# First pair's scan in PSUM with its sums on TensorE, the last attention in tiles and banks of its own, and another order of clearing and loading at the start

## The reference

```
h = exp(dt * A) * h + dt * B * x ;  y = sum over states of h * C ;  y = (y + x * D) * silu(z)
```

## Time and profile before

| | us |
|---|---|
| median of 3 runs | 2176.59 (2176.43 to 2183.86) |
| the profiled execution | 2186.44 |
| its span | 2184.6 |

### The profile page before, as it was taken

The page is one execution under the profiler, slowest core; times in us unless marked ns, Lnnn a source line. Parts: engine busy times, 40 slices in busy tenths (PEclk is TensorE's granted clock), DMA queues, the critical chain, the costliest instruction groups (busy, mean ns, idle before and its releaser), DMA issues.

```text
span 2184.6 us, 17479 instructions
## 1 busy us (share of the span) xinstructions
PE 1713.5 (78%) x6245; PEld 983.5 (45%) x6245; DVE 1372.9 (63%) x1516; ACT 651.0 (30%) x983; POOL 1016.5 (47%) x708
## 2 busy tenths in 40 slices
PE   2024354347999987999999979999998899999885
PEld 1011121014564543665555635655465466664552
DVE  3497799954467996648899956568997300124224
ACT  1003133112424333333344333423532322222210
POOL 1788855877752347775643477863343000000000
PEclk7556565568999997899999979999999799999557
DMA  8453202023531132343311332432121012210000
GB/s 167 110 140 95 63 20 70 24 75 104 132 101 35 44 82 64 88 116 87 97 46 52 81 95 86 114 95 77 29 58 44 0 44 63 54 44 10 1 0 10
DMA packets 174926, 148.43 MB, mean 68 GB/s; under 512 B 137972, under 2 KB 138360, under 8 KB 174840
## 3 DMA queue, kind: packets, MB, share of 16 engines
q1 hardware_dynamic: 147192, 71.78, 13.7%
q0 software_dynamic: 27648, 75.53, 12.2%
HBM read 132.01 MB, written 15.24 MB: 67 GB/s over the span
## 4 chain that ended last, share of the span: by engine, by line
PE 54%; DVE 23%; issue 5%; ACT 4%; DMA 1%; POOL 0%; DVEq 0%; SPq 0%; ACTq 0%; POOLq 0%
PE ps L801 39%; PE ps L804 10%; DVE tiles L1387 4%; DVE tiles L1380 4%; DVE tiles L1395 3%; DVE slot L1334 2%; PE ps L1016 2%; DVE slot L1338 1%; PE ps L846 1%; DMA mring<-mixing 1%; ACT tiles L619 1%; DVE sampled L1345 1%; ACT tiles L716 1%; ACT tiles L621 1%; DVE normal L1278 1%
## 5 line engine op out<-in xcount | busy, mean ns | idle before, releaser
L565 POOL DMA_INDIRECT slot<-corners,index x576 | 723.1, 1255 | 271.3 <-issue 163.3
L801 PE MATMUL ps<-toep,tiles 128*128 128x512 f32 (+3 forms) x2048 | 589.6, 436 | 4.2 <-DMA mring<-mixing 1.9
L801 PEld LDWEIGHTS ps<-toep,tiles 128*128 128x128 f32 x2048 | 368.8, 191 | 232.1 <-issue 134.0
L581 POOL TENSOR_TENSOR tiles<-tiles 128x1024 f32<-128x1024 f32 x120 | 291.3, 2427 | 355.9 <-DVE tiles L1387 343.0
L1387 DVE TENSOR_TENSOR_SCAN tiles<-tiles 128x1024 f32<-128x1024 f32 x128 | 301.2, 2353 | 12.3
L700 ACT COPY tiles<-ps 128x512 f32<-128x512 f32 x256 | 149.6, 585 | 466.3 <-PE ps L801 466.0
L801 PE MATMUL ps<-tiles,sel 96*128 96x512 bf16 x512 | 162.7, 442 | 137.6 <-DVE tiles L1395 116.1
L804 PE MATMUL ps<-tiles,mring 128*128 128x128 f32 (+2 forms) x1024 | 243.8, 381 | 0.0
L801 PE MATMUL ps<-tiles 128*128 128x64 f32 (+5 forms) x770 | 197.1, 401 | 36.1 <-ACT tiles L716 17.6
L685 ACT ACTIVATE tiles<-tiles,negA 128x1024 f32<-128x1024 f32 x128 | 146.8, 1149 | 233.6 <-DVE tiles L1387 212.7
L804 PEld LDWEIGHTS ps<-tiles,mring 128*128 128x128 f32 x1024 | 167.2, 191 | 77.5 <-issue 66.0
(11 more groups left out here) (231 smaller groups left out, 1772.6 us busy)
## 6 DMA issues: line engine op xcount, KB each, us to landing
toep<-in_phi_pad_dram SPq DMA_DIRECT2D x64, 513.0 KB, 4.0
mring<-mixing SPq DMA_DIRECT2D x128, 128.0 KB, 4.4
slot<-corners,index POOLq DMA_INDIRECT x576
corners<-turned SPq DMA_DIRECT2D x128, 64.0 KB, 1.9
corners<-tiles SPq DMA_DIRECT2D x4, 648.0 KB, 4.9
residual<-in_x_dram SPq DMA_DIRECT2D x4, 512.0 KB, 3.9
mixing<-tiles SPq DMA_DIRECT2D x8, 256.0 KB, 4.5
out_dram<-residual SPq DMA_DIRECT2D x4, 512.0 KB, 2.7
```

Source lines behind the costliest of these rows:

```text
L565: g.indirect_dma_start(out=slots[number % 3][:, k, :, :].rearrange("p a c -> p (a c)"), out_offset=None, in_=tables[h], in_offset=bass.Ind ...
L581: g.tensor_tensor(f(Y[h]), f(Y[h]), f(HC[n % 2]), ALU.add).then_inc(*ysum.up())
L801: return t.matmul(o, w, r, start=start, stop=stop)
```

## The change

- **The beginning.** VectorE clears only the two tiles that serve as zeros for the tables, and the offset weights; POOL clears all other weight tiles before its first gather. SyncE loads x, constants, offset weights and bias, fills the tables with zeros, writes the tables of pair 0 as soon as x is turned, and only then loads mixing weights and all the rest. ScalarE loads its function table before the first wait. Folding the convolution taps into `win` is a unit of its own, one setup step earlier.
- **Scan of pair 0.** The input product is written over the B row in ps[2], and the scan reads it there. TensorE adds the products HC into ps[0] by multiplying with the identity, and finish_y reads ps[0]. The B row of the next state waits for the scan, not for the input product. VectorE's order is scan s, product s, input s+1. POOL does nothing for this scan. Pairs 1 to 3 are as before.
- **Heads.** Exp, Ln and step sizes are done by halves of 512 columns, and the x projection of a half waits only for its own half of the convolution.
- **Last attention.** D of pair 3 becomes stage E with buffers and semaphores of its own: ps[0] and ps[1], tiles 0 to 5, 10, 18 and 19. It waits for its own layer norm alone.
- **Order.** TURNS is written anew for all engines. On POOL pair 0 and pair 1 gather in one run (A288), then come the 32 sums of pair 1. On VectorE seven groups of pair 1 (two before) stand ahead of the last finish_y of pair 0. On TensorE, D of pair 2 goes on behind the spectral stage of pair 3, interleaved with E: at "variance 3" of pair 3, blocks 0 to 10 of pair 2's 16 row blocks have been begun and the rest follows (before, all of them and its experts up to the thirteenth were ahead). The units between the marks in the middle are the same, in another interleaving.

```diff
-        A122 B A3 B A3 B A4 B A4 B A4 B A4 B10 A4 B A3 B A B A B A B A B A B A B A B A B A B A B A B A2 B A122 B32 A123 B
+        A288 B32 A121 B A3 B A B A B A6 B A4 B A4 B A4 B25 A124 B A2 B4 A10 B A4 B A4 B25""",
...
             for s in range(N_STATE * h, N_STATE * h + N_STATE):
+                if j == 0:
+                    pe += [("b rows", j, s), ("c rows", j, s)] + ([("sum", j, s - 1)] if s % N_STATE else [])
+                    dve += [("scan", j, s), ("product", j, s)]
...
+        def in_place(j):
+            return j == 0
...
+        attentions = (Attention(0, 0, 6, 7, 8, (11, 12), 13, 15, 16, 17, 9, ps[2], ps[3]),
+                      Attention(1, PAIRS - 1, 0, 1, 2, (3, 4), 19, 10, 3, 18, 5, ps[0], ps[1]))
...
+            load(xs(0)[:], x_v[0], xin_in)
             load(cst[:], consts, early)
-            load(xs(0)[:], x_v[0], xin_in)
+            for h, r in enumerate(image):
+                load(F[r, 16, 0:TAPS * 18].rearrange("p (k o) -> p k o", o=18), w_off, early)
             load(boff[:], bcast_row(b_off), early)
             sp.wait_ge(*zeroed.at(0, 1))
...
             def load_rest():
+                sp.wait_ge(*weights_zeroed.at(0, 1))
+                for tile, m in ((0, M_plus), (4, M_minus)):
+                    load(...)
...
+            for tile in (wmain, win, wout, wqkv2, wqkv3, wrouter, wexp, bexp, mar, mring[0], mring[1]):
+                g.memset(tile[:], 0.0)
+            for n in range(2):
+                last = g.memset(normal[n][:, 0:2], 0.0)
+            last.then_inc(*weights_zeroed.up())
             pool.wait_ge(*ready.at(0, 1))
...
-                pe.wait_ge(*x1_ok.at(j, 2 * h + 2))
+                pe.wait_ge(*x1_ok.at(j, 2 * h + q + 1))
...
+                read = scan_ok if in_place(j) or s == 0 else bin_ok
+                if some(read.at(j, s)):
+                    pe.wait_ge(*read.at(j, s))
                 wide(ps[2], sel[:, n, :], bcs[h]).then_inc(*b_ps.up())
...
+            def sum_states(j, s):
+                h, n = s // N_STATE, s % N_STATE
+                pe.wait_ge(*hc_ok.at(j, s + 1))
+                if n == 0 and h == 1:
+                    pe.wait_ge(*y2_ok.at(j, 1))
+                for q in range(2):
+                    last = t.matmul(sums[:, HALF * q:HALF * q + HALF], ident, F[:, HC[n % 2], HALF * q:HALF * q + HALF],
+                                    start=n == 0, stop=n == N_STATE - 1, skip_group_check=True)
+                last.then_inc(*first_sum.up())
...
             def query_or_key(j, n):
                 if n == 0:
                     pe.wait_ge(*ld1.ok.at(j, 1))
                     if j + 1 < PAIRS:
                         pe.wait_ge(*y2_ok.at(j + 1, 2))
-                    else:
-                        pe.wait_ge(*out_ok.at(j - 1, 1))
...
-                v.tensor_tensor(f(DBX[s % 2]), f(DTX[s // N_STATE]), ps[2][:], ALU.mult).then_inc(*bin_ok.up())
+                to = ps[2][:] if in_place(j) else f(DBX[s % 2])
+                v.tensor_tensor(to, f(DTX[s // N_STATE]), ps[2][:], ALU.mult).then_inc(*bin_ok.up())
...
-                v.tensor_tensor_scan(f(HS), f(DA[s % 2]), f(DBX[s % 2]), 0.0, ALU.mult, ALU.add).then_inc(*scan_ok.up())
+                given = ps[2][:] if in_place(j) else f(DBX[s % 2])
+                v.tensor_tensor_scan(f(HS), f(DA[s % 2]), given, 0.0, ALU.mult, ALU.add).then_inc(*scan_ok.up())
```

More of the change, by code:

```diff
@@ L85, in at, with __init__, up @@
     def at(self, j, n):
-        return self.sem, j * self.per_pair + n
-STAGES = "AHBCD"
+        return self.sem, (j - self.first) * self.per_pair + n
+class Part:
+    def __init__(self, event, earlier):
+        self.event, self.earlier = event, earlier
+    def up(self):
+        return self.event.up()
+    def at(self, j, n):
+        return self.event.at(j, self.earlier + n)
+STAGES = "AHBCDE"
 BANK_UNITS = ("fold", "average", "turn x", "offsets", "turn offsets", "turn", "turn last", "conv samples", "x in", "z in", "rows", "step",
@@ L99, in one_of_each, with place_of @@
     return [(name, j, 0) for name in names]
+def place_of(j):
+    return 1 if j == PAIRS - 1 else 0
 class Plan:
@@ L113, in __init__ @@
             self.spectral(j, *(of[e]["C"] for e in ("PE", "DVE", "ACT", "SP")))
-            self.attention(j, *(of[e]["D"] for e in ("PE", "DVE", "ACT", "SP")))
+            self.attention(j, *(of[e]["DE"[place_of(j)]] for e in ("PE", "DVE", "ACT", "SP")))
         self.stages = of
@@ L142, in sampling @@
                 act += [("copy last", j, m // 2)]
+            if j == 0 and m == 4:
+                dve += [("fold taps", 0, 0)]
             if j == 0 and 1 <= m <= 6:
@@ L157, in heads @@
             pe += both("x in") + both("z in") + both("rows") + both("step")
-            act += both("silu x") + both("silu z") + both("copy rows") + both("soft") + [("exp ln", j, h)]
-            dve += both("split rows") + [("step sizes", j, h)]
+            act += both("silu x") + both("silu z") + both("copy rows")
+            for q in (2 * h, 2 * h + 1):
+                act += [("soft", j, q), ("exp ln", j, q)]
+            dve += both("split rows") + both("step sizes")
     def scan(self, j, pe, dve, act, pool):
@@ L1106, in work @@
                     c_rows(j, m)
+                if unit == "sum":
+                    sum_states(j, m)
                 if unit == "out":
@@ L1167, in _ @@
             boot = lambda ins: (ins.then_inc(*boot_v.up()), dve.wait_ge(*boot_v.at(0, boot_v.raised)))
-            for tile in (woff, wmain, win, wout, wqkv2, wqkv3, wrouter, wexp, bexp, mar, mring[0], mring[1]):
-                v.memset(tile[:], 0.0)
-            v.memset(F[:, 17:19, :], 0.0)
+            v.memset(F[:, 17:19, :], 0.0).then_inc(*zeroed.up())
+            v.memset(woff[:], 0.0).then_inc(*zeroed.up())
             v.memset(eps, 1.0e-5)
-            for n in range(2):
-                last = v.memset(normal[n][:, 0:2], 0.0)
-            last.then_inc(*zeroed.up())
+            dve.wait_ge(*zeroed.at(0, 2))
             dve.wait_ge(*early.at(0, early.raised))
@@ L1392, in product @@
                 dve.wait_ge(*c_ps.at(j, s + 1))
-                if some(ysum.at(j, s - 1)):
-                    dve.wait_ge(*ysum.at(j, s - 1))
-                v.tensor_tensor(f(Y[h]) if n == 0 else f(HC[n % 2]), f(HS), ps[3][:], ALU.mult).then_inc(*hc_ok.up())
+                if some(summed(j, s - 1)):
+                    dve.wait_ge(*summed(j, s - 1))
+                to = f(Y[h]) if n == 0 and not in_place(j) else f(HC[n % 2])
+                v.tensor_tensor(to, f(HS), ps[3][:], ALU.mult).then_inc(*hc_ok.up())
             def finish_y(j, h):
-                dve.wait_ge(*ysum.at(j, N_STATE * (h + 1)))
-                link(v.scalar_tensor_tensor(out=f(Y[h]), in0=f(XC[h]), scalar=dskip, in1=f(Y[h]), op0=ALU.mult, op1=ALU.add))
+                dve.wait_ge(*summed(j, N_STATE * (h + 1)))
+                link(v.scalar_tensor_tensor(out=f(Y[h]), in0=f(XC[h]), scalar=dskip, in1=sums[:] if in_place(j) else f(Y[h]),
+                                            op0=ALU.mult, op1=ALU.add))
                 v.tensor_tensor(f(Y[h]), f(Y[h]), f(SZ[h]), ALU.mult).then_inc(*y2_ok.up())
```

399 lines of the change are left out of this document (212 added, 187 removed).

## The result

The changed kernel takes 2108.52 us (median of 4 runs, 2099.8 to 2110.8) where the kernel before, run beside it, takes 2180.23 (2176.43 to 2183.99): a ratio of 0.9664, 95% interval 0.9628 to 0.97, or 71.7 us less. The forecast was 2080, 98 us less, with a range of 2040 to 2128; the narrower range that it gave its own mechanism, 2060 to 2100, was missed.

What follows compares the result with a forecast made beforehand. VectorE was taken to bound the first pair, TensorE the middle, a chain of dependent short steps the last attention. +3 - 36 + 0 - 41 - 24 = -98 us against the median 2176.59 gave 2079, rounded to 2080; range 2040 to 2128.

Steps and rivals of the forecast that it cites:

- -36: First spectral stage, between first and second output projection: becomes bound by TensorE, 349 against 384.7 us; bounds 0 and -50.
- -41: Pair 3's saturated spectral stage: shortens as 38 to 48 us of pair 2's attention work on TensorE moves behind it.
- 0 for the middle: Two middle periods, 837.4 to 1683.5 us: same units, only interleaving and halved heads change; bounds -20 and +15.
- the halved heads: Before the first scan: x projection needs half the convolutions, 2 us; halved softplus steps 1 us; first scan step near 194.5.
- the 13 us for late B rows: First pair's scan: B rows queue behind sums on TensorE, 0.4 us per state over 32 states; bounds 0 and 29.
- the guess from the product rows: First pair's scan: a PSUM operand costs nothing, as for the input product (1202 ns with, 1225 without).
- the step given: First spectral stage: pair 1's gathers start near 330, end near 550, its scan near 710, so TensorE bounds the stage.
- -24: Last normalisation to the end: two attention streams in separate banks and tiles take 152 us against 175.9; bounds 125 and 199.
- rival (a): The tail keeps 1.2 GHz and the two streams hinder each other in queues: 199 instead of 152, total 2127; chance 0.13.

Runs made afterwards that it cites:

- the repeat: The changed kernel run again with no edit, beside the kernel before: 2107.45 us, ratio 0.9665.
- both kinds of useless matmuls: Changed kernel plus two overwritten matmuls ahead of each turn of probabilities in the end: 512 columns wide 2093.38 us (0.959), 64 columns 2081.67 us (0.9523).
- the lonely end: Pair 3's attention alone behind its spectral stage, in the kernel with the old-order end (2141.31 us); two wide useless matmuls ahead of each turn there: 2156.17 us, 0.9876.

## Why the prediction came out as it did

**Sign and size** held for three terms of the sum: -36, -41, and 0 for the middle were measured at -41, -46 and +6. Of thirteen profiled executions with the changed middle eleven have 851 to 852 us there and two have 847.3 and 847.9. The kernel before has 846.1 in the one execution that was profiled, so whether its 5 us are a cost of the change is open. **The total** came out in its range with help from errors that offset each other: the first pair, the first spectral stage and the saturated one came out 21.8 us better than forecast in sum, the middle and the end 33.2 us worse.

**The beginning.** The prediction's main claim, that the early gathers are worth nothing because VectorE still waits for the last weight load at about 93, is confirmed by the trace (94.11) and by the run with the old beginning. Small terms were wrong: the first scan step came at 198.8, not 194.5 (197.4 before), so the halved heads, counted at 3 us, saved nothing that shows; no run took them out by themselves. The clearing on POOL is done at 7.5 us; one of its rows gives 0.9 us for 1,024 columns, within my bounds of 0 to 18:

```profile
5.58 1.83 POOL L655 MEMSET mring<- 128x1024 f32 x2
```

**The first pair.** Forecast 456, measured 443.7. The term that failed is the 13 us for late B rows: 0.6 us was waited. I had weighed TensorE between half and full clock, 0.4 us late per state; with the sums on TensorE the granted clock there is 0.79 (0.56 with them on GpSimd again), and the B row hides behind scan and product. Without that term the sum was 443. That this is the measured time is partly luck: the scan began 4 us later than forecast, and from there to the projection it took 245 us instead of 248. The scan from PSUM costs 2285 ns against 2290 from SBUF in the run that puts it back (2328 in the changed kernel's other pairs): the guess from the product rows was right, and the fixed cost for a PSUM source that the Trainium skill (VectorE: DVE Perf Modes, the errata section) gives does not show. What I missed is that the place of the scan's operand matters to POOL and not to VectorE: the run with the scan in SBUF is 5 to 10 us later at the projection, by gather issues that stand under the scan. Nor did I see how much hangs on the sums leaving GpSimd's queue: 63 to 66 us at the projection in this order of VectorE's work, in the better of two orders. A part of that is VectorE's own work, which the forecast took over from the rows of before: up to the first projection its weighting took 3282 ns each before the change, 2547 in the changed kernel, and 3022 and 2982 in the two runs with the sums back on GpSimd, while the scans stayed at 2285 in both.

**The first spectral stage** took 343.6 instead of 349, and the traces agree with the step given: pair 1's last gather was issued at 577.67, 67 us earlier than before though not by my 550 (a group took 15.2 us from its first gather at 334.26, not 13.8), and TensorE was busy 266.0 of 282.3 us behind the head. No run undid this reordering by itself, so its 41 us are read from traces and not shown by an experiment.

**The last two attentions.** The -41 for the saturated stage was right (-45.7; -44.5 by the run that undoes it alone). **The step that failed is the one behind it, -24, measured +3.4**, and +7 in the repeat. The prediction had said that it would be wrong if the end took as long as before, and it did. The term rested on the clause that the second stream lifts the clock, by which the first 114.7 us would shrink to 72 (TensorE's 93.3 us at a granted 0.54 would fall by 43, to 50; the prediction gives the 72 as if it were TensorE's). The second stream did close the gaps, to 50.96 us busy of 51.0, and the clock still stood at 0.50. That was rival (a), given 0.13; its 199 us were too many, and the granted clock is 0.81 to 0.89 in the other parts of the end. The runs with useless matmuls show that the clock is the larger part of the cause: at a granted 1.00 or 0.91 in the same 50 us the end takes 169.2 and 162.1 us.

At 162 it is still 10 above my 152, so of the 31 us between forecast and repeat (182.8 - 152) the clock is at least 21. About 3 of the other 10 are the last part, which I had let shrink from 61 to 58: from the write that adds pair 3's context it took 57.9 us before and 58.4 to 58.7 in the changed kernel, its repeat and both runs with useless matmuls. The rest I put down to two streams that stand in each other's way in one queue, and to a clock that is still below 1.00 in parts; no run shows either by itself.

I had cited the Trainium skill (TensorE: Matmul & The Clock Gate, HAM oscillation) for idle gaps as the cause of the slow clock. The trace after shows that the clock can stay down without them: the profile, which models the ends of matmuls, has none to speak of in the slow stretch. The same page (Part 4: PE-mode transpose) says that transposes do not count as busy in the way that other matmuls do. In the 50 us from 1950 the changed kernel ran 50 transposes (42 of L1095, 8 of L1110) among some 165 recorded matmuls; its three largest groups there:

```profile
L872 PE MATMUL ps<-tiles 128*128 128x64 f32 x90 | 20.1, 413 | 0.0
L872 PE MATMUL ps<-tiles 64*128 64x512 f32 x12 | 11.7, 1111 | 0.0
L1095 PE MATMUL ps<-cst,tiles 128*128 128x128 f32 x42 | 11.7, 431 | 0.0
```

That would fit both kinds of useless matmuls, which stand next to transposes and are none. It does not explain the lonely end, where wide ones changed nothing. No run here separates transposes from other short matmuls, and what makes the clock stay down there is open. Shown is only that the stretch can be at either level with nearly the same program, and what the end takes in each case.

## What to carry to other kernels

Read the granted clock beside the busy share: a stretch at full busy and half clock looks saturated and is not, and a few cheap matmuls beside the real ones may be worth it (14 and 26 us here, by the medians); whether they are must be tried, since in one place here they cost 15. When work leaves a stage where one engine is saturated, count that gain by itself, and put no gain on the overlap that it is moved into until a run shows one (here -24 was forecast and +3 to +7 came); and give what is moved its own tiles and banks first, or the overlap is a queue (here 84 us). The place of an operand on one engine can set how long another engine's instructions take (here gather issues of 1.83 us instead of 0.95): look at the other engine's durations before calling a move free.

## What the runs showed of the hardware

- TensorE stood at half clock for 50 us while it was busy 50.96 of 51.0 us, in two executions (0.50, 0.53). In runs with useless matmuls, 101 and 93 more ran in 50 us, and it was granted 1.00 and 0.91. In the lonely attention the wide ones left it at 0.50.
- A gather issued by GpSimd takes 0.95 us under a scan with one operand in PSUM, 1.83 us on average and up to 2.69 under the same scan from SBUF, and up to 3.23 under the weighting of two SBUF tiles in the changed kernel.
- Up to the first projection VectorE's weighting takes 2547 ns each in the changed kernel, where GpSimd does no additions, and 3022 and 2982 in the two kernels where it does (3282 before the change).
- A scan of 128x1024 with one operand in PSUM takes 2285 ns, from SBUF 2290 in the same place and 2328 in the other pairs: no cost.
- GpSimd clears 1,024 fp32 columns in 0.9 us, where its two-operand add of as many takes 2.4.
